# Graph layer: the node search's block gathers and the score scatters moved ahead of the first column of row gathers on POOL

## The reference, cut to what matters

```
h = x @ W_gat                                   # 7744 nodes, 4 heads x 4
e = leaky_relu(a_src[src] + a_dst[dst])         # one score per edge and head
ee = exp(e - segment_max(e, dst)[dst])
agg = segment_sum(h[src] * ee / denom[dst], dst)
scores = layernorm(agg + b).mean(heads); two best of 4 experts, softmax of their scores
out = sum over experts of gate * (gelu(x @ W1 + b1) @ W2 + b2)
```

## Time and profile before

| | us |
|---|---|
| Median of 3 runs | 13642.95 (13641.0 to 13647.71) |
| Profiled execution | 13640.96 |
| its span | 13639.1 |
| Block with the row gathers (first to last of POOL's, L2811) | 10406.2 to 13217.4 |
| POOL: 1152 row gathers, busy | 1126.4 |
| PE, whole span, busy | 10483.9 |
| DVE, whole span, busy | 9129.2 |

### The profile page before, as it was taken

The page is one execution under the profiler, slowest core; times in us unless marked ns, Lnnn a source line. Parts: engine busy times, 40 slices in busy tenths (PEclk is TensorE's granted clock), DMA queues, the critical chain, the costliest instruction groups (busy, mean ns, idle before and its releaser), DMA issues. The chain is left out here.

```text
span 13639.1 us, 199791 instructions
## 1 busy us (share of the span) xinstructions
PE 10483.9 (77%) x63293; PEld 7441.6 (55%) x63293; DVE 9129.2 (67%) x31844; ACT 5339.6 (39%) x12790; POOL 1374.1 (10%) x1365
## 2 busy tenths in 40 slices
PE   2596799985977999999999999998923164455553
PEld 2486577763863555555555555557913154455543
DVE  7656787665777888888888888876657133233335
ACT  2463466652544555555555555554500000000000
POOL 0000000000000000000000000000002624433331
PEclk6797899997988999999999999998956576677776
DMA  0000000000003444443443444430012412111112
GB/s 5 4 1 2 11 1 4 1 4 2 1 7 88 97 102 101 97 103 100 97 102 100 98 102 100 99 88 2 1 29 54 21 24 33 27 29 24 29 27 61
DMA packets 442935, 640.64 MB, mean 47 GB/s; under 512 B 156927, under 2 KB 397024, under 8 KB 421355
## 3 DMA queue, kind: packets, MB, share of 16 engines
q1 hardware_dynamic: 376993, 563.52, 17.1%
q0 software_dynamic: 45920, 29.04, 2.8%
q10 hardware_dynamic: 19008, 35.69, 0.9%
HBM read 390.28 MB, written 47.31 MB: 32 GB/s over the span
## 5 line engine op out<-in xcount | busy, mean ns | idle before, releaser
L1812 PE MATMUL pm_out<-pm_w,pm_tab 128*128 128x484 f32 x8192 | 3997.1, 569 | 0.2 <-DVE pm_w L2056 0.2
L1917 ACT ACTIVATE pm_e<-pm_sums 128x484 f32<-128x484 f32 x4096 | 2319.7, 574 | 1370.5 <-PE pm_sums L1827 1351.6
L2056 DVE SCALAR_TENSOR_TENSOR pm_w<-pm_sums,pm_e 128x484 f32<-128x484 f32 x4096 | 2675.7, 654 | 85.1 <-ACT pm_e L1917 71.5
L1812 PEld LDWEIGHTS pm_out<-pm_w,pm_tab 128*128 128x128 f32 x8192 | 1558.7, 191 | 1008.8 <-issue 733.5
L1827 PE MATMUL pm_sums<-pm_mv,pm_pick 96*128 96x484 bf16 x4096 | 1508.9, 369 | 20.1 <-DMA pm_mv<-pm_parts 20.1
L2966 DVE TENSOR_TENSOR g_picked<-g_lookup,g_mask 128x1024 f32<-128x1024 f32 x112 | 137.1, 1224 | 1851.4 <-issue 1774.5
L2854 PE MATMUL g_lookup<-ed_parts,h 121*128 121x128 bf16 x10752 | 727.9, 226 | 742.8 <-issue 722.2
L2811 POOL DMA_INDIRECT g_got<-gat_sources,ed_idx x1152 | 1126.4, 978 | 1453.1 <-DVE g_msg L3061 1085.4
L2854 PE MATMUL g_lookup<-ed_parts,g_onehot 121*128 121x128 bf16 x10752 | 745.9, 228 | 605.2 <-issue 566.7
L2854 PEld LDWEIGHTS g_lookup<-ed_parts,h 121*128 121x128 bf16 x10752 | 650.1, 101 | 818.7 <-issue 795.6
L2854 PEld LDWEIGHTS g_lookup<-ed_parts,g_onehot 121*128 121x128 bf16 x10752 | 665.2, 102 | 684.8 <-issue 644.0
(11 more groups left out here) (592 smaller groups left out, 19066.8 us busy)
## 6 DMA issues: line engine op xcount, KB each, us to landing
pm_tab<-in_L_ffn_tables SPq DMA_DIRECT2D x128, 2048.0 KB, 7.9
pm_mv<-pm_parts SPq DMA_DIRECT2D x3072, 60.5 KB, 2.4
pm_gb<-pk_threshold_rows SPq DMA_DIRECT2D x128, 242.0 KB, 7.6
g_spread_low<-gat_low_rows ACTq DMA_DIRECT2D x112, 242.0 KB
gat_running<-g_rec SPq DMA_DIRECT2D x16, 1536.0 KB
g_got<-gat_sources,ed_idx POOLq DMA_INDIRECT x1152
gat_expert_rows<-g_y ACTq DMA_DIRECT2D x32, 242.0 KB
g_y<-gat_expert_rows SPq DMA_DIRECT2D x4, 1936.0 KB
```

Source lines behind the costliest of these rows:

```text
L1812: pe.matmul(out[:, hd % 2, 0:CHUNK], tab[hd % 2][:, t, :], w[:, t % NW, :], start=(t == 0), stop=(t == KT - 1)).then_inc(used, 1)
L1917: a.activation(e[:, t % NW, :], sums[:, t % NB, 0:CHUNK], ACT.Exp).then_inc(exp_ready, 1)
L2056: v.scalar_tensor_tensor(out=w[:, t % NW, :], in0=sums[:, t % NB, 0:CHUNK], scalar=0.0, in1=e[:, t % NW, :], op0=ALU.is_gt, op1=ALU.mult). ...
```

## The change

```
-                SEARCH, SCATTER = 24, 40
+                SEARCH, SCATTER = 0, 0
```

## The result

The changed kernel takes 13694.71 us (median of 7 runs, 13687.63 to 13706.89), the kernel before beside it 13644.63 us (7 runs, 13639.81 to 13651.33). The difference is 50.1 us, the ratio 1.0038 with an interval of 1.0026 to 1.0049. The change makes the kernel slower by more than the 27 us that a measurement can tell. The profiled execution of the changed kernel took 13704.36 us, at the upper end of its runs, so its trace shows 63 us more than the trace of before.

A forecast was written before the change was run, and what follows sets the result against it. The prediction took the stage as a sum of POOL's gather stretches, where PE crawls, and PE's groups. +54.9 (gathers, tail, less PE's work) - 4.9 (`blk`) - 4 (round trip) = +46 us gave 13688 us, range 13672 to 13703.

The forecast's parts named there:

- The 40 gathers were hidden, and are exposed now: POOL's 24 gathers before the search and 16 before the scatters cost nothing there; in the long burst they add 51.4 us.
- PE crawls while POOL gathers: PE during POOL's row gathers: 2.8 us a matmul instead of 0.057, so longer bursts delay PE's groups and all that follows.
- 2 KB block gathers: The search's gathers: claimed not to slow PE to any such degree, with 1342 matmuls in their 130 us.
- The 40 gathers, predicted at 1.285 us each: Growth of POOL's long burst after the scatters: 51.4 us, between 50.0 and 56.0.
- The tail: PE's crawl continuing after the long burst ends: about 0.12 us an instruction, so +4.6 us (0 to +5.6).
- `blk`: Input the search waits for: DVE's five gaps among its pivot counts vanish, so it comes 4.9 us earlier (0 to -4.9).
- The round trip of the starts: Storing starts and loading ends before the scatters: shorter without 16 gathers in flight, -4 us (0 to -15).
- what PE gets done in the longer crawl: PE in the added burst time: 20 matmuls, worth 1.1 us, taken off the cost.
- all later bursts keep their length: POOL's later bursts of 72 gathers: same number and size as before, so no change in length.
- the block ends 46 us later: End of the block with the row gathers: delayed by the forecast's whole sum, +46 us.
- Rival 1: POOL's idle 151.5 us before the first `msg` absorbs the 40 gathers; about -9 us, 13634; chance 0.14.
- Rival 2: The long burst costs more than in proportion, POOL falling into the slow pace earlier; +70 us, 13713; chance 0.12.

The follow-up runs named there:

- r2: The changed kernel again, on chip 7 without the crawl: 12507.78 us against 12456.5 for the kernel before, +51.3 us, ratio 1.0040.
- e1: Changed kernel with the first 40 of chunk 0's row gathers left out (set to zero), chip 2: 12450.87 against 12447.02 us for the kernel before, ratio 1.0002.
- e2: Against the kernel before, only the search moved ahead of the first 24 row gathers, which join the long burst, chip 2: 12481.93 us, +34.9, ratio 1.0027.
- e3: Against the kernel before, only the scatters moved ahead of the 16 row gathers in the starts' round trip, chip 2: 12462.82 us, +15.8, ratio 1.0013.
- e4: Against the kernel before, 16 more row gathers put in the round trip of the starts, ahead of the scatters, chip 2: 12432.47 us, -14.6, ratio 0.9989.
- e5: Against the kernel before, 16 more row gathers ahead of the search and 15 more in the starts' round trip, chip 7: 12417.78 us, -38.7, ratio 0.9971.
- e8: Kernel before plus a POOL pause (128x256 tensor_tensor) after each row gather, chip 6, one run: 13007.88 against 13663.51 us.
- e7: Against the kernel before, 40 row gathers ahead of the search, 30 woven into it, 31 in the starts' round trip, chip 6: 13660.52 against 13663.51 us, ratio 0.9996.
- r1: The kernel before again, unchanged, profiled on chip 7 without the crawl, one run: 12441.55 us.
- e10: Kernel before plus a 128x64 tensor_tensor pause on POOL after each row gather, chip 9 without the crawl: 12635.36 us, +191.6, ratio 1.0153.

## Why the prediction was right, point by point

**The 40 gathers were hidden, and are exposed now.** Right. Moving them behind the scatters costs 50 us on either sort of chip (result, r2). On the second sort it is shown from both sides: taking them out of the old places changes nothing (e1), moving them in two parts costs the sum (e2, e3), moving more of them into POOL's waits gives back 14.6 and 38.7 us (e4, e5). On the first sort, where the prediction was made, none of these ran; there the trace carries it, by the sizes below and by POOL's wait of 150.3 us.

**The reason given was one of two.** The prediction put the price on PE, which crawls while POOL gathers. In the trace that it read this is so. But chips 2 and 7 have no crawl and pay the same 51 us, because POOL's own queue is then the bound. In both a gather behind the scatters lengthens the stretch in which POOL issues, by 1.40 us each there (result) and 1.38 here (r2). That the totals agree so closely is partly luck: in the traces the first scatter comes 9.6 us earlier on the first sort and 6.0 us later on the second. A cause for the crawl was not given, and e8 corrects the wording "PE crawls while POOL gathers" to "while POOL issues indirect DMAs without a break". The prediction also set the 2 KB block gathers apart, since PE does 1342 matmuls beside them. But POOL waits for DVE's buffers between them (62 of them in 128.3 us), so this showed a difference of spacing as much as of kind; in e7, where two of three instructions of an unbroken run are block gathers, PE does crawl.

**The sizes.** The 40 gathers, predicted at 1.285 us each, 51.4 in all: the burst grew by 361.1 - 305.0 = 56.1 us, 1.40 each. The additional ones came at the slow pace of the burst's end, the upper bound of the term: in both traces the pace turns from 1.25 to about 1.40 some 238 us after the first scatter. The tail, predicted at +4.6: 27.3 us in both traces (10989.2 to 11016.5), so +0; it did not grow from 237 instructions to 277. The two errors, +4.7 and -4.6, cancel by luck. `blk`: -5.3 us (predicted -4.9). The search from its first to its last gather: 126.6 against 128.3 us, -1.7 (predicted 0). The round trip of the starts: 34.0 against 36.4 us, -2.4 (predicted -4). Sum in the trace +46.5 on PE's restart, where the same terms gave +47.1; and +45.3 on `msg` of chunk 0, where the prediction, with 1.1 us off for what PE gets done in the longer crawl, had +46.

**The last 4 us of the median, and 13 more in the profiled execution,** came later: `msg` of chunk 0 stands 48.2 us later than before (11136.9 against 11088.7) and that of chunk 15 63.8 us later (13486.1 against 13422.3), 2.86 of each from the start. POOL's twelve other waits for `msg` grew by 22.4 us together, while the twelve bursts between them took 7 us less together (90.1 to 93.8 us each in either trace). Why PE took longer between them in this execution is open; "all later bursts keep their length" was right to within 4 us, "the block ends 46 us later" was short for this one.

**The round trip has no rule that I can give.** On chips 2 and 7 DVE's wait for the ends was 29.7 us with no row gather in it (e3), 34.6 and 38.1 with 16 (r1, e2), 43.3 with 32 (e4), 49.0 with 31 (e5), but 41.0 with none in r2 and e1, where the search comes first. So the gain of -4 that was taken for emptying it has the other sign in r2, and what else sets it is open.

**The rivals.** Rival 1, absorbed in POOL's idle 151.5 us, fell by the wait of 150.3 us. Rival 2, a burst that costs more than in proportion, is right in one point: each of the 40 cost 1.40, not 1.285. But POOL did not fall into the slow pace earlier, and the tail did not grow. The Trainium skill says in "SBUF — State Buffer" (the list under the picture of its two sides) that engine and DMA ports are disjoint and that PE never waits on anyone there. On chip 7 the trace agrees with what the prediction drew from this, 3167 matmuls in 227 us beside 167 instructions of POOL; on the chip of the prediction and on chip 6 it does not, and e8 shows that the slowdown there goes with how POOL issues. No run shows by what path POOL holds PE up.

## What to carry to other kernels

An engine's idle time says nothing about whether work on it can be moved. Ask of each stretch what the others do meanwhile: gathers were free where POOL waited for DVE, and full price where POOL's issuing was the length of the stretch. Put independent work ahead of a wait, not behind it, and fill the wait to its length (e5). And if another engine stands at "issue" for as long as POOL issues indirect DMAs back to back, try to space them: on such a chip a pause of 256 columns took 655.6 us off (e8, one run), on one without the effect the pause of 64 columns added 191.6 (e10), so look at the traces of more than one chip first.

## What was not expected of the hardware

- While POOL issued indirect DMAs without a break, every 1.25 to 1.40 us, PE issued one matmul in 2.80 us on the chips of the first sort. On the others it kept 0.057 to 0.059 us, for the same instructions, with POOL at 1.25 us in some stretches and 1.35 on average. With a pause and 1.84 us between them PE kept up on a chip of the first sort too.
- The size of the rows does not decide it: scatters of 16 bytes a row brought the crawl in e8, row gathers of 80 bytes in the trace of before, and runs with two of three gathers at 2 KB a row brought it in e7. DVE showed gaps too, 0.64 to 1.35 us, at the end of the first 24 gathers (prediction).
- The chips differ in this by 1200 us of 13650 for one program, and what makes a chip of one sort or the other was not found.
- A row gather with an eighth of the rows still takes 0.84 us of POOL (median) in place of 0.94.
